# Attention plus routed feed-forward on one core: query and key stacks turned by DMA instead of by TensorE, with a fourth score bank and a new order of work

## Chip, cores and metric

One core of one Trainium2 chip. The metric is the device time of one execution in microseconds, the median of several runs. Before the change it is 717.38 us (three runs, 717.0 to 717.58).

## The reference, cut to what matters

x is 16 batches of 128 tokens with 512 numbers each; the context has 16 x 128 rows of 256.

```python
def xattn(x, ctx, pos):                      # 32 heads of 16
    q = rope(x @ Wq, pos); k, v = split(ctx @ Wkv); k = rope(k, pos)
    w = softmax(einsum('bqhd,bkhd->bhqk', q, k) / sqrt(16))
    return einsum('bhqk,bkhd->bqhd', w, v).reshape(b, n, 512) @ Wout + bout
def ffn(x):                                  # 16 experts of 352, the best 2 taken, and a shared one
    return shared(x) + sum(combine[:, e] * swiglu(x, w1[e], w3[e], w2[e]) for e in range(16))
x = x + xattn(layernorm(x), ctx, pos)
x = x + ffn(layernorm(x))
```

## The kernel before, in words

The kernel has two stages. The first handles attention, one batch of 128 tokens after the other. The second is the feed-forward part: 16 shared tiles of 128 rows, then the rows sorted by expert. The change is in the first stage, and in what the second takes over from it.

Every factor of a product in half precision is held as two f16 numbers, a high part and a low part, whose sum is the f32 value. A projection (`product`, L485) is therefore three matmuls for each 128 rows of depth. For the scores the same is done in another way. Each head has 16 numbers; `parts` holds for each head a stack of 64: for a query head high, low, high, low, for a key head high, low, low, high. The product of the two stacks over depth 64 gives all four partial products at once. The stacks lie with the tokens on the partitions and must be turned, so that the depth lies on the partitions: two heads (2 x 64) make one block of 128 x 128. There are 16 blocks for the queries and 16 for the keys of a batch.

How the stacks come about before the change, for each batch:

- `q_turn`, `q_sum` and `k_turn`, `k_sum` (VectorE, L1067 to L1091) apply the rotary embedding from the PSUM bank `p_qk` into `rot`.
- `q_high`, `k_high` (ScalarE, L793, L800) write the high part, 128x512. `q_low`, `k_low` (GpSimd, L1461 and L1466) write the low part, 128x512.
- `q_double`, `k_double` (GpSimd, L1471 and L1477) copy both parts to their second places: one instruction of 128x1024, and two of 128x512.
- `stack_transpose` (TensorE, L524), four times a batch, turns 8 blocks into the bank `p_st`. `qT_copy` twice and `kT_copy` once (ScalarE, L807, L813) and `kT_copy` once (VectorE, L1093) take them from there into `qT` and `kT`, 128x1024 each.

Then `scores` (L539) forms the scores of 8 heads at a time in two PSUM banks, `row_max` (VectorE, L1099) takes the row maxima, `negmax_transpose` (L554) turns them, `shifted_scores` (L559) forms the scores again, turned and with the maximum subtracted, `exp` (ScalarE, L820) writes the probabilities, `weigh_values` (L574) multiplies them with the values and sums them, `sums_invert` and `normalise` (VectorE, L1114, L1120) divide, and `project_out` (L601) applies Wout. The scores go through three banks: bank 0 for all even groups of heads, banks 1 and 2 by turns for the odd ones (`p_scored`, L289). So a pair of groups must wait until the pair before it has left bank 0.

The order of the work is written out by hand. Each engine has a function `step(b, on)`, and `on(d, part)` runs a part for batch b+d. `pipeline` (L297) calls it for b = 0, 1, 2, ... (from 6 on as a loop). The engines work through their lists in order and wait for each other by semaphores. Before the change TensorE is at batches b to b-4 in one step, with the scores of a batch begun at the end of step b+1 and finished in step b+2. SyncE issues the loads of the context and the stores of the normalised rows and their turned copies (`store_xn2`, `store_xn2T`).

`qT`, `kT` and `parts` exist once, so turning batch b+1 has to wait until `shifted_scores` of batch b has read the same half of `qT` and `kT`.

## Time and profile before

| | |
|---|---|
| median of three runs | 717.38 us (717.0 to 717.58) |
| the profiled execution, its own time | 722.21 us |
| its span, first to last instruction | 720.2 us |
| mean granted TensorE clock in it | 0.987 of full speed |
| attention stage, until the last output projection | about 357 us |
| feed-forward stage | about 363 us |
| PE / DVE / ACT / POOL busy, share of the span | 94% / 73% / 55% / 51% |

PE is TensorE's matmuls, PEld its weight loads, DVE VectorE, ACT ScalarE, POOL GpSimd, SP SyncE; a q behind an engine (SPq) is its queue of DMA issues. A row of a group gives the line, the engine, the operation, what is written and read, how often, the busy time and the mean of one, and then how long the engine sat idle before it and who released it. Matmuls of TensorE overlap, so the time that a block of them takes is read from the start of the block to the start of the next one, not from its duration.

### The profile page before, as it was taken

How to read it: one execution, taken by the hardware profiler on the slowest of the kernel's cores; microseconds unless marked ns; L12 is line 12 of the kernel's file. 1: busy time of each engine (PE TensorE's matmuls, PEld its weight loads, DVE VectorE, ACT ScalarE, POOL GpSimd, SP SyncE). 2: the span in 40 equal slices, each digit the busy share in tenths (PEclk: the TensorE clock that was granted, in tenths of full speed). 3: DMA queues.
4: the chain of work that ended last, by engine and by line, in shares of the span. 5: the costliest groups of instructions: out<-in, count | busy, mean ns of one | idle time of the engine just before them, and what ended most of it. 6: DMA issues, size and time to landing. Idle time of an engine off the chain costs nothing.

```text
span 720.2 us, 20582 instructions
## 1 busy us (share of the span) xinstructions
PE 675.9 (94%) x7616; PEld 435.0 (60%) x7616; DVE 522.3 (73%) x992; ACT 399.7 (55%) x668; POOL 365.9 (51%) x438
## 2 busy tenths in 40 slices
PE   3589999999999999998999999999999899999992
PEld 1356666666666666666655656666666466666661
DVE  8678888888888888876647773776767567667671
ACT  4365566666666656657531111666666456666661
POOL 4645655565556655554200001355765667777662
PEclk9999999999999999999999999999999999999997
DMA  8440111100001110100032274286587774445952
GB/s 281 174 137 1 39 39 40 39 36 17 28 30 36 36 36 29 58 29 32 32 117 88 75 278 153 74 232 165 105 261 222 207 206 86 82 85 107 263 114 32
DMA packets 37698, 73.89 MB, mean 103 GB/s; under 512 B 4048, under 2 KB 8144, under 8 KB 37648
## 3 DMA queue, kind: packets, MB, share of 16 engines
q1 hardware_dynamic: 26736, 48.81, 19.4%
q0 software_dynamic: 8752, 20.71, 15.2%
q10 hardware_dynamic: 2160, 3.69, 1.7%
q8 instruction: 33, 0.54, 0.3%
q14 instruction: 17, 0.14, 0.1%
HBM read 69.85 MB, written 22.81 MB: 129 GB/s over the span
## 4 chain that ended last, share of the span: by engine, by line
PE 83%; DMA 7%; DVE 3%; issue 3%; POOL 1%; ACT 1%; POOLq 0%; SPq 0%; DVEq 0%
PE p_sc L717 13%; PE p_qk L686 12%; PE p_st L686 11%; PE p_v L488 9%; PE p_qk L488 8%; PE p_pv L588 5%; PE p_st L536 4%; PE p_pv L591 4%; PE p_sc L568 3%; PE p_sc L551 3%; PE p_pv L598 2%; PE p_tr L680 2%; DMA stream<-x 2%; PE p_pv L704 2%; PE p_sc L571 2%
## 5 line engine op out<-in xcount | busy, mean ns | idle before, releaser
L824 ACT ACTIVATE prob<-p_sc 128x512 f32<-128x512 f32 x128 | 71.4, 601 | 53.7 <-PE p_sc L571 53.7
L1105 DVE TENSOR_REDUCE negmax<-p_sc 128x4 f16<-128x512 f32 x128 | 82.6, 684 | 6.2 <-PE p_sc L551 5.6
L946 ACT CAST hiddenT<-p_pv 128x384 f16<-128x384 f32 x54 | 25.9, 479 | 106.6 <-PE p_pv L704 104.1
L1510 POOL COPY from_at<-from_rows 128x1 uint32 (+1 forms) x40 | 33.3, 833 | 81.1 <-DVE from_rows L1351 77.8
L1530 POOL DMA_INDIRECT out<-prob,to_at x38 | 68.5, 1803 | 11.5 <-issue 10.9
L717 PE MATMUL p_sc<-used_twice,hiddenT 128*128 128x512 f16 (+1 forms) x306 | 72.9, 384 | 1.0 <-DVE hiddenT L1236 1.0
L686 PE MATMUL p_qk<-used_twice,xeT 128*128 128x352 f16 x420 | 68.4, 313 | 0.6 <-DMA xeT<-xn2T_dram 0.6
L686 PE MATMUL p_st<-used_twice,xeT 128*128 128x352 f16 x420 | 68.4, 312 | 0.0
L1232 DVE TENSOR_TENSOR hidden<-p_st,act_g 128x352 f32<-128x352 f32 x55 | 28.8, 524 | 52.9 <-PE p_st L686 32.4
L931 ACT COPY xeT<-p_tr 128x1024 f16<-128x1024 f16 x40 | 40.5, 1012 | 36.9 <-PE p_tr L680 34.3
L1249 DVE TENSOR_SCALAR prob<-p_sc,gate_at 128x512 f32<-128x512 f32 x38 | 28.6, 751 | 37.3 <-PE p_sc L717 33.8
L686 PEld LDWEIGHTS p_st<-used_twice,xeT 128*128 128x128 f16 x420 | 40.9, 98 | 21.3
L1491 POOL TENSOR_TENSOR xn_parts<-xn,xn_parts 128x512 f16<-128x512 f32 x16 | 18.5, 1158 | 69.0 <-ACT xn_parts L851 69.0
L588 PE MATMUL p_pv<-prob,used_twice_too 128*32 128x128 f32 x1024 | 52.8, 278 | 0.5 <-DVE attn L1124 0.5
L686 PEld LDWEIGHTS p_qk<-used_twice,xeT 128*128 128x128 f16 x420 | 40.8, 98 | 19.4 <-DMA xeT<-xn2T_dram 0.9
L591 PE MATMUL p_pv<-prob,sum_row 128*32 128x128 f32 x1024 | 51.7, 274 | 0.0
L488 PE MATMUL p_qk<-used_twice,xnT 128*128 128x512 f16 x192 | 49.1, 380 | 1.3 <-DVE swp L1077 1.3
L1515 POOL DMA_INDIRECT xe<-xn_dram,from_at x40 | 44.5, 1114 | 8.2 <-issue 4.2
L717 PEld LDWEIGHTS p_sc<-used_twice,hiddenT 128*128 128x128 f16 (+1 forms) x306 | 29.2, 98 | 31.4 <-issue 2.4
L488 PE MATMUL p_v<-used_twice,attnT 128*128 128x512 f16 x192 | 47.6, 380 | 0.5 <-POOL attnT L1487 0.5
L536 PE MATMUL p_st<-ident,used_twice 128*128 128x128 f16 x512 | 40.0, 222 | 7.2 <-DVE used_twice_too L1097 3.8
L1463 POOL TENSOR_TENSOR used_twice<-rot,used_twice 128x512 f16<-128x512 f32 x16 | 18.6, 1165 | 53.4 <-ACT used_twice L798 53.4
(188 smaller groups left out, 1650.6 us busy)
## 6 DMA issues: line engine op xcount, KB each, us to landing
w<-e SPq DMA_DIRECT2D x20, 1408.0 KB
w<-e SPq DMA_DIRECT2D x20, 512.0 KB
out<-stream SPq DMA_DIRECT2D x17, 256.0 KB, 2.0
xn_dram<-xn_parts SPq DMA_DIRECT2D x16, 256.0 KB, 2.0
xn2T_dram<-xn2T SPq DMA_DIRECT2D x16, 256.0 KB, 2.0
w<-e SPq DMA_DIRECT2D x20, 192.0 KB
stream<-x SPq DMA_DIRECT2D x1, 3584.0 KB, 15.7
xeT<-xn2T_dram ACTq DMA_DIRECT2D x14, 256.0 KB, 2.7
```

Of the source, the lines that this page charges most:

```text
L488: mm = pe.matmul(to, rows[:, r_part, c, :], w[:, w_part, c, :], start=(c == 0 and r_part + w_part == 0), stop=(c == last and r_part == 1))
L536: mm = pe.transpose(p_st[:, n, :], parts[:, h:h + 2, :].rearrange("p h k -> p (h k)"), ident16[:])
L588: pe.matmul(p_pv[2 * HD * n:2 * HD * (n + 1), block], vpad[:, par, head(c, n), :], prob[:, c % RING, n * P:(n + 1) * P], start=(c % 4 == 0 ...
L591: mm = pe.matmul(pv_sum[2 * HD * n:2 * HD * (n + 1), :], sum_row[:, c % 4, :], prob[:, c % RING, n * P:(n + 1) * P], start=False, stop=(c ...
L686: mm = pe.matmul(p_out, xeT[:, u, x_part, c, :], w[:, w_part, c, at:at + INNER], start=(c == 0 and x_part + w_part == 0), stop=(c == KC - ...
L717: mm = pe.matmul(p_y[u][:], hiddenT[0:k, h_part, c, :], w[0:k, w_part, c, :], start=(c == 0 and h_part + w_part == 0), stop=(c == len(ICH) ...
L824: act.activation(prob[:, c % RING, :], p_scored(c)[:], ACT.Exp, scale=SCALE).then_inc(exp_ready, 1)
L931: act.copy(xeT[:, u], p_xT).then_inc(sems.xeT_ready, 1)
L1105: dve.tensor_reduce(negmax[:, c % 2, at:at + CH], p_scored(c)[:].rearrange("p (h t) -> p h t", t=P), AX_X, ALU.max, negate=True).then_inc( ...
L1510: pool.tensor_copy(from_at[:, par, u:u + 1], from_rows[:, bass.ds(q, 1)]).then_inc(from_copied, 1)
L1515: pool.indirect_dma_start(out=xe[:, u].rearrange("p a d -> p (a d)"), out_offset=None, in_=xn2_dram, in_offset=bass.IndirectOffsetOnAxis(a ...
L1530: pool.indirect_dma_start(out=out, out_offset=bass.IndirectOffsetOnAxis(ap=to_at[:, par, u:u + 1], axis=0), in_=ye[:, par, u], in_offset=N ...
```

## The change

- The bank `p_st` goes; the scores have four banks, two for each pair of groups, by turns. The shared feed-forward part's `p_u` moves to the fourth score bank. The turned maxima go to the bank `p_tr`, which the layernorm turns of x and of xn2 use as well.
- `stack_transpose`, `qT_copy` and `kT_copy` go. SyncE issues four transposing DMAs for each batch in their place, each 128 x 1024 f16 (256 KB), straight from `parts` to `qT` or `kT`.
- `q_high`, `k_high`, `q_low`, `k_low` write each number to both of its places at once (128x1024 out of 128x512 read twice); `q_double` and `k_double` go.
- The load of x from batch 2 on, and the loads of the shared expert's weights, are issued by ScalarE.
- The steps of all engines have a new order. Scores of a batch are taken two steps behind, shifted scores and values three, the output projection four.

The core of the diff:

```diff
-        p_st32 = ps("p_st", [P, 512])
-        p_sc = [ps(f"p_sc{n}", [P, CH * P]) for n in range(3)]
+        p_sc = [ps(f"p_sc{n}", [P, CH * P]) for n in range(4)]
+        p_neg = p_xT[:, 0, 0, :]
+        p_g, p_u, p_hT = p_qk[:, 0:INNER], p_sc[3][:, 0:INNER], p_pv[:, 0:len(ICH) * P]
...
         def p_scored(c):
-            return p_sc[1 + c // 2 % 2 if c % 2 else 0]
+            return p_sc[c // 2 % 2 * 2 + c % 2]
...
+            def turn_parts(b, par, to, ready, parts_ready, at, half):
+                sp.wait_ge(parts_ready, b + 1)
+                if later(b, 1):
+                    sp.wait_ge(shifted, b * (NCH // 2) - (2 - 2 * half))
+                sp.nop().then_inc(turning, 1)
+                heads = slice(at + HALF * half, at + HALF * (half + 1))
+                sp.dma_start_transpose(to[:, 8 * half:8 * half + 8, :], parts[:, heads, :].rearrange("p h k -> p (h k)")).then_inc(ready[half], 16)
...
             def step(b, on):
-                on(4, load_ctx)
-                on(-1, store_xn2)
-                on(-1, store_xn2T)
+                on(-2, turn_k_parts, 0)
+                on(-2, turn_q_parts, 0)
+                on(-5, store_xn2)
+                on(1, load_ctx)
+                on(-2, turn_k_parts, 1)
+                on(-5, store_xn2T)
+                on(-2, turn_q_parts, 1)
...
             def scores(b, par, cc):
                 if cc % 2 == 0:
-                    pe.wait_ge(qT_ready[cc // 2], b + 1)
-                    pe.wait_ge(kT_ready[cc // 2], b + 1)
-                if cc:
-                    pe.wait_ge(max_ready, b * NCH + (2 * cc - 1))
+                    pe.wait_ge(qT_ready[cc // 2], b * 16 + 16)
+                    pe.wait_ge(kT_ready[cc // 2], b * 16 + 16)
+                if cc >= 2:
+                    pe.wait_ge(max_ready, b * NCH + (2 * cc - 2))
                 elif later(b, 1):
-                    pe.wait_ge(exp_ready, b * NCH - 1)
+                    pe.wait_ge(exp_ready, b * NCH + (2 * cc - 2))
...
             def negmax_transpose(b, par):
                 pe.wait_ge(max_ready, b * NCH + NCH)
-                pe.wait_ge(kT_ready[1], b + 1)
+                last_xn = B if isinstance(b, int) and b + 3 > B else b + 3
+                pe.wait_ge(xnT_lo, last_xn)
...
             def shifted_scores(b, par, cc):
...
-                else:
-                    pe.wait_ge(exp_ready, b * NCH + (2 * cc - 1))
+                elif cc >= 2:
+                    pe.wait_ge(exp_ready, b * NCH + (2 * cc - 2))
```

The order of TensorE after the change, one step (d is the batch b+d): project_out(-4) 0 and 1, project_k(-1) 1, negmax_transpose(-3), project_out(-4) 2, shifted_scores(-3) 0 and 1, project_out(-4) 3, weigh_values(-3) 0 and 1, shifted_scores(-3) 2 and 3, project_q(-1) 0, spread_recip(-3) 0, project_q(-1) 1, scores(-2) 0 and 1, weigh_values(-3) 2 and 3, project_q(-1) 2 and 3, xn2_transpose(-4), project_v(-1) 0, spread_recip(-3) 1, scores(-2) 2 and 3, gate_logits(-4), project_v(-1) 1, xn_transpose(0), project_k(0) 0.

VectorE: row_max(-3) 4 to 7, q_sum(-2), xnT_low(-1), neg_copy(-3), ln1_stats(0), k_turn(-1), residual(-4), ln2_stats(-4), ln1_norm(0), sums_invert(-3) 0, k_sum(-1), normalise(-3) 0, ln2_norm(-4), row_max(-2) 0 to 3, sums_invert(-3) 1, q_turn(-1), normalise(-3) 1.

ScalarE: xnT_copy(-1), q_high(-2), exp(-3) 0 to 3, summed_v_copy(-3) 0, exp(-3) 4 to 7, xn2_high(-4), summed_v_copy(-3) 1, ctx_high(0), k_high(-1), xn2T_copy(-4), attnT_high(-3), keep_logits(-4), v_copy(-1).

GpSimd: attnT_low(-4), q_low(-2), rstd1_make(0), rstd2_make(-4), xn2_low(-4), bias_add(-2), ctx_low(0), k_low(-1).

```diff
-                act.copy(parts[:, 0:HEADS, 0:HD], rot[:, 0:DIM].rearrange("p (h d) -> p h d", d=HD)).then_inc(q_hi, 1)
+                act.copy(q_part[:, :, :, 0, :], twice_each(rot[:, 0:DIM])).then_inc(q_hi, 1)
...
-                pool.tensor_tensor(parts[:, 0:HEADS, HD:2 * HD], rot[:, 0:DIM].rearrange("p (h d) -> p h d", d=HD), parts[:, 0:HEADS, 0:HD],
-                                   ALU.subtract).then_inc(q_lo, 1)
+                pool.tensor_tensor(q_part[:, :, :, 1, :], twice_each(rot[:, 0:DIM]), q_part[:, :, :, 0, :], ALU.subtract).then_inc(q_parts, 1)
```

## Rows read from the trace of the kernel before

**Rows 1.** The page, busy time of engines: us, share of the span, instructions.

```profile
PE 675.9 (94%) x7616; PEld 435.0 (60%) x7616; DVE 522.3 (73%) x992; ACT 399.7 (55%) x668; POOL 365.9 (51%) x438
```

**Rows 2.** Busy time of engines by stretches, with granted clock, DMA share, GB/s.

```profile
core 0: us, PE busy (x) PEld busy (x) DVE busy (x) ACT busy (x) POOL busy (x), PEclk, DMA share, GB/s
...
32.00:52.00 20.00, 16.75 (x227) 9.89 (x225) 15.22 (x31) 13.01 (x23) 9.05 (x8) 0.91 0.34 116
52.00:331.00 279.00, 278.67 (x4523) 184.26 (x4520) 234.83 (x477) 176.03 (x304) 162.15 (x149) 1.00 0.09 33
...
357.00:720.20 363.20, 344.75 (x2426) 218.86 (x2424) 231.05 (x399) 180.71 (x295) 171.43 (x237) 0.98 0.56 146
```

**Rows 3.** The same view for one batch of the steady stretch.

```profile
200.00:220.00 20.00, 20.00 (x326) 13.25 (x325) 17.02 (x36) 12.56 (x22) 11.75 (x12) 1.00 0.09 33
```

**Rows 4.** The timeline of TensorE: start, us, line, operation, count.

```profile
204.23 0.23 PE L568 MATMUL p_sc<-used_twice_too 64*128 64x128 f16 x2
...
204.78 0.43 PE L588 MATMUL p_pv<-prob,used_twice_too 128*32 128x128 f32 x8
...
205.79 0.62 PE L536 MATMUL p_st<-ident,used_twice 128*128 128x128 f16 x8
206.34 0.23 PE L568 MATMUL p_sc<-used_twice_too 64*128 64x128 f16 x2
...
215.55 0.40 PE L551 MATMUL p_sc<-used_twice_too 64*128 64x128 f16 x8
215.88 0.82 PE L488 MATMUL p_v<-used_twice,ctx 128*128 128x512 f16 x3
216.54 0.61 PE L598 MATMUL p_pv<-recip,spread_to 128*128 128x128 f32 x4
```

**Rows 5.** Groups by line and shape, 100 to 300 us (ten batches).

```profile
L1105 DVE TENSOR_REDUCE negmax<-p_sc 128x4 f16<-128x512 f32 x80 | 52.0, 685 | 2.8 <-PE p_sc L551 2.4
L824 ACT ACTIVATE prob<-p_sc 128x512 f32<-128x512 f32 x80 | 44.7, 600 | 35.3 <-PE p_sc L571 35.3
...
L1475 POOL TENSOR_TENSOR used_twice<-used_twice,ones 128x1024 f16<-128x1024 f16 x10 | 21.3, 2134 | 0.8
L811 ACT COPY used_twice_too<-p_st 128x1024 f16<-128x1024 f16 x20 | 20.7, 1037 | 0.0
...
L1463 POOL TENSOR_TENSOR used_twice<-rot,used_twice 128x512 f16<-128x512 f32 x10 | 11.7, 1167 | 33.5 <-ACT used_twice L798 33.5
...
L1487 POOL TENSOR_TENSOR attnT<-attn,attnT 128x512 f16<-128x512 f32 x10 | 11.6, 1156 | 5.0 <-ACT attnT L836 5.0
...
L1097 DVE COPY used_twice_too<-p_st 128x1024 f16<-128x1024 f16 x10 | 6.9, 692 | 5.1 <-PE p_st L536 4.9
...
L798 ACT CAST used_twice<-rot 128x512 f16<-128x512 f32 x10 | 6.2, 618 | 2.0 <-DVE rot L1087 2.0
```

**Rows 6.** The page, DMA queue (packets, MB, share) and issues (KB each, us to landing).

```profile
q1 hardware_dynamic: 26736, 48.81, 19.4%
...
xn2T_dram<-xn2T SPq DMA_DIRECT2D x16, 256.0 KB, 2.0
...
stream<-x SPq DMA_DIRECT2D x1, 3584.0 KB, 15.7
xeT<-xn2T_dram ACTq DMA_DIRECT2D x14, 256.0 KB, 2.7
```

**Rows 7.** The timeline of TensorE: first scores of batches 0, 1, 15; last output projection.

```profile
32.09 0.51 PE L551 MATMUL p_sc<-used_twice_too 64*128 64x128 f16 x8
...
52.07 0.40 PE L551 MATMUL p_sc<-used_twice_too 64*128 64x128 f16 x8
...
331.09 0.40 PE L551 MATMUL p_sc<-used_twice_too 64*128 64x128 f16 x8
...
354.65 2.76 PE L488 MATMUL p_v<-used_twice,attnT 128*128 128x512 f16 x12 [0.17 <-POOL attnT L1487]
```

More of the change, by code:

```diff
@@ L283, in build, with twice_each @@
         attn_rows = attn[:].rearrange("p a n -> p (a n)").rearrange("p (c t) -> p c t", t=P)
+        q_part = parts[:, 0:HEADS].rearrange("p h (t u d) -> p h t u d", t=2, u=2)
+        k_part = parts[:, HEADS:2 * HEADS]
+        k_hi_part = bass.AP(k_part.tensor, k_part.offset, [k_part.ap[0], k_part.ap[1], [3 * HD, 2], [1, HD]])
+        k_lo_part = k_part[:, :, HD:3 * HD].rearrange("p h (t d) -> p h t d", t=2)
+        def twice_each(rows):
+            return rows.rearrange("p (h o d) -> p h o d", o=1, d=HD).broadcast_to([P, HEADS, 2, HD])
         def head(c, n):
@@ L661, in step @@
-                on(-1, stack_transpose, 0)
-                on(-2, shifted_scores, 3)
-                on(-2, spread_recip, 0)
-                on(0, xn_transpose)
-                on(-1, stack_transpose, 2)
-                on(-1, scores, 0)
-                on(-2, weigh_values, 2)
-                on(-2, weigh_values, 3)
-                on(0, project_v, 0)
-                on(-1, stack_transpose, 3)
-                on(-1, scores, 1)
-                on(0, project_v, 1)
-            pipeline(step, pe, 0, B + 1, 6, (B - 6) // 2, ahead=[xn_transpose])
+                if isinstance(b, int) and b == B + 2:
+                    pe.wait_ge(turned_q, B * 3)
+                    pe.wait_ge(lo13, KC)
+                    gate(0, 0, 0, 0, "shared")
@@ L676, in rows_transpose @@
+                on(-4, xn2_transpose)
+                on(-1, project_v, 0)
+                on(-3, spread_recip, 1)
+                on(-2, scores, 2)
+                on(-2, scores, 3)
+                if isinstance(b, int) and b == B + 2:
+                    pe.wait_ge(exp_ready, B * NCH)
+                    up(0, 0, 0, 0, "shared")
+                on(-4, gate_logits)
+                on(-1, project_v, 1)
+                on(0, xn_transpose)
+                on(0, project_k, 0)
             def rows_transpose(n, u, j):
@@ L802, in k_high @@
                 if later(b, 1):
-                    act.wait_ge(stacked[1], b)
-                    act.wait_ge(stacked[3], b)
-                act.copy(parts[:, HEADS:2 * HEADS, 0:HD], rot[:, DIM:2 * DIM].rearrange("p (h d) -> p h d", d=HD)).then_inc(k_hi, 1)
-            def qT_copy(b, par, half):
-                act.wait_ge(stacked[2 * half], b + 1)
-                if later(b, 1):
-                    act.wait_ge(shifted, b * (NCH // 2) - (2 - 2 * half))
-                act.copy(qT[:, 8 * half:8 * half + 8, :], p_st[:]).then_inc(qT_ready[half], 1)
-            def kT_copy(b, par):
-                act.wait_ge(stacked[3], b + 1)
-                if later(b, 1):
-                    act.wait_ge(shifted, b * (NCH // 2))
-                act.copy(kT[:, 8:16, :], p_st[:]).then_inc(kT_ready[1], 1)
+                    act.wait_ge(kT_ready[0], b * 16)
+                    act.wait_ge(kT_ready[1], b * 16)
+                act.copy(k_hi_part, twice_each(rot[:, DIM:2 * DIM])).then_inc(k_hi, 1)
             def exp(b, par, c):
@@ L873, in split_shared2 @@
             def split_shared2():
-                for g in range(4):
-                    act.wait_ge(stacked[g], B)
+                act.wait_ge(qT_ready[0], B * 16)
                 for c, (i, k) in enumerate(ICH):
@@ L1091, in k_sum @@
                 dve.tensor_tensor(rot[:, DIM:2 * DIM], rot[:, DIM:2 * DIM], swp[:, DIM:2 * DIM], ALU.add).then_inc(k_rot, 1)
-            def kT_copy(b, par):
-                dve.wait_ge(stacked[1], b + 1)
-                if later(b, 1):
-                    dve.wait_ge(shifted, b * (NCH // 2) - 2)
-                dve.tensor_copy(kT[:, 0:8, :], p_st[:]).then_inc(kT_ready[0], 1)
             def row_max(b, par, c):
@@ L1189, in step @@
             def step(b, on):
-                on(-2, q_turn)
+                on(-3, row_max, 4)
+                on(-3, row_max, 5)
+                on(-3, row_max, 6)
+                on(-3, row_max, 7)
                 on(-2, q_sum)
+                on(-1, xnT_low)
+                on(-3, neg_copy)
+                if isinstance(b, int) and b == B + 2:
+                    split_shared13((0, 1))
                 on(0, ln1_stats)
+                on(-1, k_turn)
                 on(-4, residual)
-                on(-2, kT_copy)
                 on(-4, ln2_stats)
```

170 lines of the change are left out of this document (62 added, 108 removed).

## The prediction

> **What bounds the kernel now.** I read the page's busy shares first: TensorE is busy 94% of the span, VectorE 73% [rows 1]. A share over the whole span mixes stages, so I cut it into stretches: from 52 to 331 us TensorE is busy 278.67 of 279 us at the full clock (2.4 GHz), and the DMA engines are nearly idle, 0.09 [rows 2]. One batch there takes 20.0 us, with 17.02 us of VectorE, 12.56 of ScalarE and 11.75 of GpSimd [rows 3]. The timeline shows TensorE going from block to block without gaps [rows 4]. So the attention stage is bound by TensorE, and VectorE comes next, 3 us behind. The feed-forward stage, from 357 us on [rows 2], gets the same instructions as before (one bank has another name); I leave its 363 us alone.
>
> **What goes.** A block of eight stack turns starts at 205.79 and the next block at 206.34: 0.55 us [rows 4]. There are four a batch, 2.2 us in all. On TensorE nothing covers them: they leave the bound itself. VectorE loses one copy of 0.69 us (L1097), ScalarE three of about 1.03 (L811 and its like), GpSimd 2.13 (L1475) and two of about 1.15, as L1463 is [rows 5].
>
> **What comes on ScalarE and GpSimd.** A high part now writes 1024 numbers from 512. The nearest rows are 0.62 us for 512 (L798) and 1.04 for 1024 (L811) [rows 5]; I take the upper, so two cost 0.8 us more, and ScalarE stands at 12.6 - 3.1 + 0.8 = 10.3 us a batch. A low part on GpSimd lies between 1.17 (L1463) and 2.13 (L1475); the upper again: 11.75 - 4.4 + 1.9 = 9.2 us. Both are hidden under TensorE's 17.8 and cost nothing by themselves.
>
> **The transposing DMAs.** The trace has none, and they decide the case. Four of 256 KB a batch. Lower bound: a plain 256 KB store lands 2.0 us after issue, a load of 256 KB into SBUF 2.7, and a long load needs 15.7 us for 3584 KB, which is 1.12 us for each 256 KB that follows another [rows 6]. So two in a row land after 2.7 + 1.1 = 3.8 us. Upper bound: a turned block has rows of 128 f16, 256 bytes; one DMA has 8 blocks x 128 rows = 1024 such rows, 64 for each of 16 DMA engines. If each row costs what a packet costs in this trace on average (19.4% of 16 x 720.2 us over 26736 packets = 84 ns [rows 6]), one DMA needs 5.4 us. I take the plain transfers, because size, queue and memory are the same and only the order of the bytes differs; the upper end stays for the range.
>
> The Trainium skill, "DMA: Bandwidth & Descriptors", section "Latency and other measured facts", gives 261 GB/s as the measured effective rate of DMA transposes; by an estimate from it 256 KB take 1.0 us, and the sum would stay as it is; no row here has such a DMA. The same skill speaks against the change in "VectorE: DVE Perf Modes", section "The three transpose paths": 390 ns for a 128x128 turn on TensorE and 1309 ns by the crossbar DMA; eight turned one after the other would by that estimate take 10.5 us a DMA, and no row here shows this either.
>
> **Do they fit in the order?** I walk one step after the change; durations from rows 3 to 5, zero is the step's start. TensorE: two parts of the projection and one of k (0.66 each, 215.88 to 216.54 [rows 4]) to 2.0; turned maxima; shifted scores 0 and 1 (0.55 each, 204.23 to 204.78) end at 3.8; values 0 and 1 (1.0 each) at 6.5; shifted 2 and 3 at 7.6; scores 0 of the next batch start at 9.4. SyncE may turn k half 0 only when shifted 1 is done (`turn_parts`), about 4.0, and q half 0 when GpSimd's low part is ready: high part from 1.0 to 2.0 on ScalarE, low part to 4.2. Both must land by 9.4, so they have 5.4 us; the plain price of 3.8 fits with 1.6 to spare. The other halves start at 7.8 and are needed at 15.0, which is looser. With a fixed part of 0.9 and D for each DMA the deadline is met up to D = 2.2 us. Each us beyond that comes twice into every step.
>
> **What is queued behind these waits.** On SyncE the stores of normalised rows, the stores of their turned copies and the context load stand behind the DMA that waits for shifted scores. The context is wanted at 12.8 of the next step, and ScalarE's next copy of turned rows at about 14, while the store goes out at 9 and lands in 2.0 [rows 6]: both cost nothing while D stays small. ScalarE issues the load of x at about 9 us, before the first copy of the layernorm; half a us of issue is covered by VectorE's weight splits.
>
> **What is late next.** VectorE now holds 17.02 - 0.6 = 16.4 us in a step of 17.8. My walk gives three near misses: the maxima's turn waits for `xnT_low`, done at 1.7, with TensorE there at 2.0; the projection waits for the low part of attnT on GpSimd (1.16 us [rows 5]), which ends about 0.3 us ahead; the first values wait for exp 1 (0.60 us each, L824 [rows 5]), which ends 0.1 us late, and exp 3 0.2 us late. The fourth score bank lets scores 0 and 1 run back to back and takes nothing off TensorE's own work. For the short waits I add 0.25 us a step: 20.0 - 2.2 + 0.25 = 18.05, say 18.1 us a batch.
>
> **The sum.** The first scores of batch 0 stand at 32.09 and those of batch 15 at 331.09 [rows 7]: 15 periods of 19.93 us. 15 x (19.93 - 18.1) = 27.5 us. At the start the old order needs 20.0 us from the scores of batch 0 to those of batch 1 [rows 7]; in the new one batch 1's scores need only finished exps of batch 0, some 15 us later by the same walk (8 us to the turned maxima, 6.7 from there to scores 0), so of the 3 us I take 2 more. From the scores of batch 15 to the last projection it is 23.6 us before [rows 7]; the work behind it is the same and I change nothing. 722.2 - 29.5 = 692.7 us for the profiled execution; the median of the runs stands 4.8 us under it, so **688 us**. Own range with small errors of the waits (none, or 0.7 us a step): 681 to 696.
>
> **Rivals.**
> - **VectorE becomes the bound.** Today it stands idle 3 us a batch in short waits for TensorE (17.02 of 20.0 [rows 3]). TensorE hid them; if they all stay, a step takes 16.4 + 3.0 = 19.4 us, and the gain is 15 x 0.5 = 8 us: 709. For it: row maxima (0.685 us each, eight a batch [rows 5]) and scores wait for each other twice a step. Against: four banks uncouple the pairs. Between, 696 to 713, lies a good part of the chance.
> - **Turned scores come late: slower.** Place: TensorE's wait on `qT_ready[0]` and `kT_ready[0]` ahead of scores 0. At D = 5.4 us, q half 0 lands at 4.0 + 0.9 + 10.8 = 15.7 instead of 9.4, so TensorE stands 6.3 us in every step: 24.2 us a batch, 717 + 15 x 4.2 = 780 us. It decides against the change from 0.9 + 2D = 5.4 + 1.9, so D = 3.2 us. Pauses also cost clock: with waits of about 2 us TensorE's granted clock was 0.91 from 32 to 52 us [rows 2], that is, part of it at 1.2 GHz. The crossbar figure of the Trainium skill's VectorE page would belong here, beyond 780.
> - **It does not do what it says:** the DMA writes turned numbers one by one, 131072 of two bytes. Even at a tenth of a packet's 84 ns that is 69 us a DMA on 16 engines, over 1000 us in all. For it speaks no row; the plain store of 256 KB in 2.0 us speaks against any such pace.
>
> **Chances.** A measurement of this kernel can tell about 0.2% (1.4 us) from no change. Forecast 0.50 (681 to 696), VectorE or an unforeseen wait 0.25 (696 to 716), break-even between the sides 0.04, late turns 0.19, not as it says 0.02. So faster 0.75, same 0.04, slower 0.21. The range reaches from 680 to 712: it holds the forecast and nearly all of the second case, and what it leaves out is mostly the slower side, 2 in 10.
>
> **What would show it.** Right: blocks of L536 gone, TensorE above 97% in the steady stretch, the period between first scores about 18.1 us, ScalarE near 10 and GpSimd near 9 us in it, transposing DMAs landing in 2 to 4 us, DMA share about 0.25 (four times 256 KB beside today's 640 KB at 0.09). Wrong in the first way: TensorE idle ahead of L551 scores or the turned maxima, released by VectorE's maxima, VectorE above 90%. Wrong in the second way: idle ahead of scores released by a DMA into `qT` or `kT`, the landing times above 3.2 us, a granted clock below 1.0 in the steady stretch, and SyncE's stores late. A feed-forward stage that changes by more than 2 us would make the argument incomplete.

## The result, and the profile after

After the change the median is 691.06 us (four runs, 689.33 to 692.89) against 717.48 for the kernel before on the same chip: ratio 0.9614, 95% interval 0.9575 to 0.9653, 26 us faster. Timed once more beside the kernel before it gave 0.9667 (0.9629 to 0.9704). Forecast were 688 us and a range of 680 to 712. The profiled execution took 689.33 us, span 687.5 us, granted clock 0.984. The medians below are of all executions of a kernel; the ratios are estimated from the fast ones alone, which leaves out one execution each of e2_q_twice, e5_small_turns and e8_old_order_ctx, and they differ from the plain quotients of the medians by up to 0.4%.

The page, busy time of the engines, answers to [rows 1]:

```profile
PE 635.5 (92%) x7104; PEld 406.6 (59%) x7104; DVE 503.2 (73%) x976; ACT 368.9 (54%) x620; POOL 332.9 (48%) x390
```

TensorE has 512 matmuls fewer (16 batches x 32 turns) and 40 us less busy time. Its share fell, although it still is the bound; the shares say little here. Busy time by stretches, as in [rows 2], and one batch, as in [rows 3]:

```profile
core 0: us, PE busy (x) PEld busy (x) DVE busy (x) ACT busy (x) POOL busy (x), PEclk, DMA share, GB/s
...
32.00:52.00 20.00, 13.36 (x200) 9.13 (x201) 15.39 (x30) 11.28 (x19) 6.03 (x4) 0.83 0.29 52
52.00:300.00 248.00, 242.42 (x4098) 158.73 (x4094) 215.27 (x463) 149.63 (x262) 132.42 (x107) 1.00 0.49 104
...
325.00:690.00 365.00, 344.28 (x2414) 218.56 (x2412) 231.01 (x399) 180.62 (x294) 172.38 (x237) 0.98 0.55 146
```

```profile
204.11:221.72 17.61, 17.55 (x295) 11.46 (x293) 15.72 (x34) 11.15 (x20) 9.78 (x8) 1.00 0.43 97
```

A batch takes 17.6 us where it took 20.0. VectorE fills 89% of it and still doesn't hold TensorE up. In the fill, 32 to 52 us, TensorE does less than before (13.36 us against 16.75). The feed-forward stage is as it was.

The timeline of TensorE, first scores of batches 0, 1 and 15 and the last output projection, as in [rows 7]:

```profile
30.86 0.62 PE L552 MATMUL p_sc<-used_twice_too 64*128 64x128 f16 x16 [0.38 <-DMA used_twice_too<-used_twice]
...
51.22 0.62 PE L552 MATMUL p_sc<-used_twice_too 64*128 64x128 f16 x16
...
298.37 0.88 PE L552 MATMUL p_sc<-used_twice_too 64*128 64x128 f16 x16
...
322.63 2.76 PE L504 MATMUL p_v<-used_twice,attnT 128*128 128x512 f16 x12 [0.33 <-POOL attnT L1450]
```

This gives the balance of the two spans (720.2 - 687.5 = 32.7 us). The first scores stand 1.2 us earlier. The 15 periods to the scores of batch 15 went from 19.93 to (298.37 - 30.86) / 15 = 17.83 us: 31.5. From there to the last projection it is 24.3 us against 23.6: -0.7. Behind it lie 364.9 against 365.5: +0.7. So the whole gain is the shorter period. (The two profiled executions lie 6.3 us further apart than the two medians, so 32.7 us is more than the 26 of the medians, and no trace tells in which stage the difference lies.) But the first of these periods, batch 0 to 1, is 20.4 us long; in the steady part ten of them (105.13 to 282.33) take 17.72 each.

Inside a step, the timeline of TensorE from 204 us, as in [rows 4] (start, us, line, operation, count):

```profile
204.91 0.23 PE L573 MATMUL p_sc<-used_twice_too 64*128 64x128 f16 x2
...
205.91 0.82 PE L504 MATMUL p_v<-used_twice,attnT 128*128 128x512 f16 x3
...
211.80 0.62 PE L552 MATMUL p_sc<-used_twice_too 64*128 64x128 f16 x16
212.35 0.43 PE L593 MATMUL p_pv<-prob,used_twice_too 128*32 128x128 f32 x8
```

Two groups of scores, 16 matmuls, now run in one block of 0.55 us. Before, each group of 8 took 0.33, as from 215.55 to 215.88 in [rows 4], so two took 0.66. Two groups of shifted scores take 1.00 us (204.91 to 205.91), before twice 0.55. With two pairs of each in a batch that is 2 x 0.11 + 2 x 0.10 = 0.4 us a batch. It stands in no term of my sum. Why a joined block is shorter, no run shows.

And the new instruction, the transposing DMA (duration on SP's queue in ns min/median/max, first and last start), with the time from issue to landing:

```profile
L425 SPq DMA_TRANSPOSE used_twice_too<-used_twice x64: 1231/1259/2214, 21.9 to 299.2; - x64
...
DMA to landing us min/median/max: 3.0/3.2/5.6
```

It holds SP's queue for 1.26 us and lands after 3.2. The first two of the step above, and a plain store for comparison, in the timeline of SP's queue:

```profile
206.09 2.62 SPq L425 DMA_TRANSPOSE used_twice_too<-used_twice  x2
209.19 0.34 SPq L405 DMA_DIRECT2D xn_dram<-xn_parts  x1
```

The second of the two, the query's half 0, is issued at about 207.4, lands by the median at about 210.6, and the scores start at 211.80. That is a slack of 1.2 us.

### The profile page after: what moved, and what is told of

Same layout as the page of the kernel before. It is cut to its first block, busy times and chain, and to the rows that moved or that the text cites. A ratio compares the mean times of both kernels' runs of the same rounds, so it can differ in the third digit from the quotient of the medians.

```text
span 687.5 us, 19434 instructions
## 1 busy us (share of the span) xinstructions
PE 635.5 (92%) x7104; PEld 406.6 (59%) x7104; DVE 503.2 (73%) x976; ACT 368.9 (54%) x620; POOL 332.9 (48%) x390
## 2 busy tenths in 40 slices
DMA packets 105279, 90.63 MB, mean 132 GB/s; under 512 B 71632, under 2 KB 75728, under 8 KB 105232
## 4 chain that ended last, share of the span: by engine, by line
PE 79%; DMA 5%; DVE 5%; issue 4%; POOL 2%; ACT 2%; SPq 2%; POOLq 0%; ACTq 0%; DVEq 0%
PE p_sc L724 14%; PE p_qk L693 13%; PE p_sc L693 12%; PE p_qk L504 8%; PE p_v L504 8%; PE p_pv L593 4%; PE p_pv L596 3%; DMA used_twice_too<-used_twice 3%; PE p_tr L687 2%; PE p_pv L711 2%; PE p_sc L552 2%; PE p_pv L603 2%; PE p_sc L573 2%; PE p_sc L576 1%; SPq L425 1%
## 5 line engine op out<-in xcount | busy, mean ns | idle before, releaser
L1085 DVE TENSOR_REDUCE negmax<-p_sc 128x4 f16<-128x512 f32 x128 | 79.4, 684 | 6.0 <-PE p_sc L552 4.6
L811 ACT ACTIVATE prob<-p_sc 128x512 f32<-128x512 f32 x128 | 66.1, 602 | 20.2 <-PE p_sc L576 19.9
L693 PE MATMUL p_sc<-used_twice,xeT 128*128 128x352 f16 x420 | 68.4, 312 | 0.0
L1211 DVE TENSOR_TENSOR hidden<-p_sc,act_g 128x352 f32<-128x352 f32 x55 | 28.8, 524 | 52.5 <-PE p_sc L693 32.0
L504 PE MATMUL p_qk<-used_twice,xnT 128*128 128x512 f16 x192 | 52.1, 399 | 6.4 <-DVE swp L1063 6.4
L1442 POOL TENSOR_TENSOR used_twice<-rot,used_twice 128x1024 f16<-128x1024 f32 x16 | 34.2, 2136 | 43.6 <-ACT used_twice L798 43.6
L693 PEld LDWEIGHTS p_sc<-used_twice,xeT 128*128 128x128 f16 x420 | 41.0, 98 | 21.4
L693 PEld LDWEIGHTS p_qk<-used_twice,xeT 128*128 128x128 f16 x420 | 40.8, 98 | 19.4 <-DMA xeT<-xn2T_dram 0.7
L724 PE MATMUL p_sc<-used_twice_too,hiddenT 128*128 128x512 f16 (+1 forms) x180 | 43.3, 386 | 0.0
```

Source lines behind the costliest of these rows:

```text
L504: mm = pe.matmul(to, rows[:, r_part, c, :], w[:, w_part, c, :], start=(c == 0 and r_part + w_part == 0), stop=(c == last and r_part == 1))
L693: mm = pe.matmul(p_out, xeT[:, u, x_part, c, :], w[:, w_part, c, at:at + INNER], start=(c == 0 and x_part + w_part == 0), stop=(c == KC - ...
L724: mm = pe.matmul(p_y[u][:], hiddenT[0:k, h_part, c, :], w[0:k, w_part, c, :], start=(c == 0 and h_part + w_part == 0), stop=(c == len(ICH) ...
L811: act.activation(prob[:, c % RING, :], p_scored(c)[:], ACT.Exp, scale=SCALE).then_inc(exp_ready, 1)
L1085: dve.tensor_reduce(negmax[:, c % 2, at:at + CH], p_scored(c)[:].rearrange("p (h t) -> p h t", t=P), AX_X, ALU.max, negate=True).then_inc( ...
L1442: pool.tensor_tensor(q_part[:, :, :, 1, :], twice_each(rot[:, 0:DIM]), q_part[:, :, :, 0, :], ALU.subtract).then_inc(q_parts, 1)
```

## The experiments

Two measures for all of them: the ratio to the kernel before, timed beside it on the same chip, with its interval, and the period, taken as the distance from the first to the last turning of the maxima (`negmax_transpose`) over 15. By that measure the kernel before has (339.2 - 38.7) / 15 = 20.03 us and the change 17.65. A period is that of the one profiled execution, which can lie several us from the median: that of the kernel before lies 4.7 us above it, those of e2, e5, e4, e8 and e9 8, 12, 7, 7 and 4 us above theirs. A few us over 15 batches are some tenths of a us of period.

| run | what it is | median us | ratio to before | period us |
|---|---|---|---|---|
| change | first timing | 691.06 | 0.9614 (0.9575 to 0.9653) | 17.65 |
| e0_change | the change, timed once more | 692.96 | 0.9667 (0.9629 to 0.9704) | 17.61 |
| e1_turns_back | change, TensorE's 32 turns back in | 713.6 | 0.9891 (0.9822 to 0.996) | 19.08 |
| e2_q_twice | change, one DMA repeated | 746.66 | 1.0365 (1.03 to 1.0431) | 21.39 |
| e3_three_banks | e6 with three banks | 735.91 | 1.0294 (1.0263 to 1.0324) | 20.91 |
| e4_dma_only | old order, three banks, doubling, DMA turns | 725.29 | 1.0072 (1.0034 to 1.0109) | 20.20 |
| e5_small_turns | change, each DMA in two halves | 738.3 | 1.0264 (1.0213 to 1.0315) | 21.15 |
| e6_wo_later | change, one weight split a step later | 688.98 | 0.9582 (0.9539 to 0.9625) | 17.81 |
| e6b_wo_later | the same again, beside e0 | 689.26 | 0.961 (0.9576 to 0.9645) | 17.79 |
| e7_double_kept | change, doubling kept | 703.76 | 0.9812 (0.9779 to 0.9845) | 18.43 |
| e8_old_order_ctx | e4, context loaded earlier | 713.36 | 0.9959 (0.9929 to 0.9989) | 19.51 |
| e9_old_order_once | e8, both places written at once | 703.66 | 0.9794 (0.9754 to 0.9834) | 18.63 |
| e10_wo_early_act | e6, ScalarE's half of the split earlier | 689.76 | 0.959 (0.9542 to 0.9639) | 17.83 |

**e1_turns_back: what are the turns worth?** Four blocks of eight turns of the identity, whose results nobody reads, are put back on TensorE.

```diff
+            def idle_turns(bank):
+                for n in range(8):
+                    pe.transpose(bank[:].bitcast(F16)[:, n * P:(n + 1) * P], ident16[:], ident16[:])
...
+                if c == 0:
+                    idle_turns(p_qk)
```

> The changed kernel with 32 turns of 128x128 a batch put back on TensorE (of the identity, into p_qk and p_v ahead of four projections, results overwritten). Theory A (the gain is the turns' own time on TensorE, the engine that bounds): a batch takes 17.7 + 2.2 = 19.9 us and the time goes to 720 to 724 us, that is, the whole gain or a little more is gone. Rival B (the gain comes from the new order and the fourth bank; the turns fit beside VectorE's work): at most 700 us.

It came out between the two: 713.6 us. The period is 1.43 us longer than the change's. A block of eight, read in the timeline of TensorE of this run:

```profile
208.30 0.62 PE L510 MATMUL p_qk<-ident 128*128 128x128 f16 x8
208.76 0.81 PE L504 MATMUL p_qk<-used_twice,xnT 128*128 128x512 f16 x3
```

That is 0.46 us, so four of them are 1.8 us of TensorE's time, of which 1.4 are seen. The turns carry most of the gain, but not all of it: with as many turns as before the kernel is still 1.1% faster (20.03 to 19.08 us). This rest is not of the new order and the fourth bank alone, for here ScalarE and VectorE still have no copies out of `p_st` to do, and GpSimd no doubling.

**e3_three_banks: is the fourth bank needed?** The version of e6 (below), with the old assignment of banks and its waits.

```diff
-            return p_sc[c // 2 % 2 * 2 + c % 2]
+            return p_sc[1 + c // 2 % 2 if c % 2 else 0]
...
-                if cc >= 2:
-                    pe.wait_ge(max_ready, b * NCH + (2 * cc - 2))
-                elif later(b, 1):
-                    pe.wait_ge(exp_ready, b * NCH + (2 * cc - 2))
+                if cc:
+                    pe.wait_ge(max_ready, b * NCH + (2 * cc - 1))
+                if cc < 2 and later(b, 1):
+                    pe.wait_ge(exp_ready, b * NCH - 1 + cc)
...
-                elif cc >= 2:
-                    pe.wait_ge(exp_ready, b * NCH + (2 * cc - 2))
+                else:
+                    pe.wait_ge(exp_ready, b * NCH + (2 * cc - 1))
```

> The kernel of the run before this one (split one step later) with three score banks in place of four: scores 1 must wait for the maxima of scores 0, shifted scores 1 and 3 for an exp each. Theory A (the fourth bank is what lets the new order put pairs of scores together): TensorE waits about 1 us behind scores 0, 1 us behind shifted 0 and as much in the other pairs, 3 to 4 us a batch, 735 to 750 us. Rival B (the bank only saves the switch between blocks, 0.1 us each): 690 to 697 us.

735.91 us, as theory A had it. What TensorE waits for between 100 and 280 us (us in total, times, longest):

```profile
PE p_sc L552 <- DVE negmax L1085: 14.3, 17, 1.1
PE p_sc L573 <- ACT prob L811: 13.1, 17, 1.1
```

The pairs stand back to back in the new order. With bank 0 shared by all even groups the second group of a pair waits for the maxima, or for the exp, of the first: 27.4 us in 180, some 3 us a batch. So the bank has no gain of its own that could be added up; it is what makes the new order possible.

**e4_dma_only, e8_old_order_ctx, e9_old_order_once: the DMA turns without the new order.** First only the turning is left to the DMAs, in the kernel before.

```diff
-                on(4, load_ctx)
-                on(-1, store_xn2)
-                on(-1, store_xn2T)
+                on(-4, store_xn2)
+                on(1, load_ctx)
+                on(-4, store_xn2T)
+                on(-1, turn_parts, kT, kT_ready, HEADS, 0)
+                on(-1, turn_parts, qT, qT_ready, 0, 0)
+                on(-1, turn_parts, kT, kT_ready, HEADS, 1)
+                on(-1, turn_parts, qT, qT_ready, 0, 1)
```

> The kernel before, with its own order, three score banks and the doubling on GpSimd kept; only the stack turns and their copies are replaced by the four transposing DMAs a batch (and the loads of x and the shared weights are issued as in the change). Theory A (the gain is the removed TensorE work, whatever the order): 17.9 to 18.3 us a batch, 685 to 697 us. Rival B (the old order and its three banks cannot use the freed time): 19.3 us or more a batch, 707 us or more.

Slower than before, 725.29 us, though TensorE has 2.2 us less to do in each batch. Both numbers are in the range of rival B, but its cause, the order and its three banks, is not what this trace shows (e8 and e9 test it). Waits from 100 to 280 us:

```profile
PE p_sc L541 <- DMA used_twice_too<-used_twice: 7.9, 8, 1.5
ACT ctx L830 <- DMA ctx_sb<-ctxT: 6.1, 9, 0.8
...
PE p_v L493 <- ACT used_twice_too L776: 4.3, 9, 0.7
```

The second row is a fault of my edit: the context load comes late, ScalarE waits for it, and the copy of the values, for which TensorE waits in the third row, comes behind. What holds the load up in SP's queue are not the transposing DMAs, as I had taken it, but the store of the normalised rows ahead of it, which waits for GpSimd. The timeline of SP's queue, first of e4, then of e8:

```profile
193.52 7.95 SPq L420 DMA_TRANSPOSE used_twice_too<-used_twice  x4
205.68 0.34 SPq L397 DMA_DIRECT2D xn_dram<-xn_parts  x1
206.31 0.41 SPq L409 DMA_DIRECT2D ctx_sb<-ctxT  x1
```

```profile
204.73 7.41 SPq L420 DMA_TRANSPOSE used_twice_too<-used_twice  x4
212.47 0.41 SPq L409 DMA_DIRECT2D ctx_sb<-ctxT  x1
216.26 0.35 SPq L397 DMA_DIRECT2D xn_dram<-xn_parts  x1
```

In e4 the last transposing DMA has left the queue at 201.5 us and the load goes out at 206.31, right behind the store. e8 issues that load a batch earlier, still behind the transposing DMAs but ahead of the store.

```diff
-                on(1, load_ctx)
...
+                on(2, load_ctx)
...
+            load_ctx(2, 0)
```

> The kernel before in its own order with its three banks and its doubling, only the turning left to the DMAs, as in the run of that name; here the context of the next batch is also loaded a step earlier, because in that run ScalarE waited 0.7 us a batch for this load, which stood behind the transposing DMAs in SP's queue. Theory A, the place of the load was what made that run no faster: 712 us or less, a period of 19.0 us or less. Theory B, the chain query parts, doubling, transposing DMA, scores is what binds in the old order, and the load was hidden or nearly so: 718 to 725 us, TensorE still waits for the transposing DMA in front of the scores, some 0.8 us a batch.

713.36 us: the late load was 1.1% of the time. The time is nearer to theory A (712 or less), the period of 19.51 us is not (19.0 or less), and the wait that theory B names is there, so both were in part right. The wait of the scores stays, at the same size:

```profile
PE p_sc L542 <- DMA used_twice_too<-used_twice: 9.9, 9, 1.4
```

One step of e8, GpSimd, then TensorE (its SP queue stands above, the four issues from 204.73 us):

```profile
204.54 1.17 POOL L1431 TENSOR_TENSOR used_twice<-rot,used_twice 128x512 f16<-128x512 f32 x1 [3.13 <-ACT used_twice L784]
205.79 2.14 POOL L1443 TENSOR_TENSOR used_twice<-used_twice,ones 128x1024 f16<-128x1024 f16 x1
...
211.30 0.40 PE L542 MATMUL p_sc<-used_twice_too 64*128 64x128 f16 x8 [0.79 <-DMA used_twice_too<-used_twice]
```

The low part of the query ends at 205.7, the doubling at 207.9, the transposing DMA issued then lands by the median 3.2 us later, at 211.1, and 0.2 us after that the scores start. e9 removes the doubling: both places are written at once, as in the change.

```diff
-                pool.tensor_tensor(parts[:, 0:HEADS, HD:2 * HD], rot[:, 0:DIM].rearrange("p (h d) -> p h d", d=HD), parts[:, 0:HEADS, 0:HD],
-                                   ALU.subtract).then_inc(q_lo, 1)
+                pool.tensor_tensor(q_part[:, :, :, 1, :], twice_each(rot[:, 0:DIM]), q_part[:, :, :, 0, :], ALU.subtract).then_inc(q_parts, 1)
...
-                on(-2, q_double)
```

> The run just named (old order, three banks, DMA turns, early context load) with both places of the parts written at once by ScalarE and GpSimd, so that no doubling stands between the query's low part and its turning. Theory A, that chain binds: it is 1.2 us a batch shorter, the wait in front of the scores goes, and the time is 705 to 715 us. Theory B, the old order binds by itself (three banks, the scores right behind the projections they depend on): the same as the run just named within 3 us.

703.66 us: theory A, a little below its range. From 100 to 280 us no scores wait for a DMA any more; the nearest are short waits of the shifted scores for an exp (1.8 us in all, 4 times). Somewhat over half of the gain of the change (2.1% of 3.3 to 3.9%) is therefore to be had in the old order with three banks: DMA turns and writing at once are worth 20.03 - 18.63 = 1.40 us a batch. From e9 to the change only the order of work and the bank differ: 18.63 - 17.65 = 0.98 us. That e1 leaves 0.95 looks like a second measure of the same, but it is of other parts, as said above, and the executions of e9 alone reach from 698.66 to 707.52 us, which would be 0.6 us a batch if it all lay in the attention stage. The two numbers agree closer than they can be known.

**e7_double_kept: writing at once, in the new order.**

```diff
+                on(-2, q_low)
+                on(-2, q_double)
...
+                on(-1, k_low)
+                on(-1, k_double)
```

> The changed kernel with the high and low parts written once and doubled on GpSimd as before (its busy time a batch 9.8 + 2.3 us, its chain from the sum to the finished parts 1.2 us longer for queries and 1.2 us longer for keys, behind which the low part of attnT stands). Theory A (writing both places at once is needed to land the turns in time: the cover was 1.2 us, and attnT's low part had 0.3 us): 0.7 to 1.5 us more a batch, 701 to 714 us. Rival B (GpSimd has 7 us to spare, so the doubling is hidden): under 694 us.

703.76 us, theory A in size. What TensorE waits for, 100 to 280 us:

```profile
PE p_v L504 <- POOL attnT L1466: 6.1, 9, 0.8
PE p_pv L593 <- ACT prob L811: 1.4, 5, 0.4
```

The wait is not where e9 has its gain. Here it is the output projection that waits, for the low part of attnT, which GpSimd reaches late behind the doubling. The same doubling hurts the query's turning in the old order and the output projection in the new one.

**e2_q_twice and e5_small_turns: how much slack have the transposing DMAs?** In e2 the first query half is turned twice, the second time after the first has landed.

```diff
+                if at == 0 and half == 0:
+                    sp.dma_start_transpose(to[:, 8 * half:8 * half + 8, :], parts[:, heads, :].rearrange("p h k -> p (h k)")).then_inc(turned_once, 16)
+                    sp.wait_ge(turned_once, b * 16 + 16)
```

> The changed kernel, but SyncE turns query half 0 twice, the second time after the first has landed. In the changed kernel that half lands about 1.2 us before TensorE starts scores 0, and a turning DMA lands 3.2 us after its issue. Theory A (scores 0 wait on that DMA once the slack is used): scores 0 come about 2 us late in every step, 19.8 us a batch, 715 to 725 us. Rival B (DMA turns have ample cover, as the walk with 1.6 us to spare and looser later halves suggests): under 695 us.

746.66 us, worse than both expectations. Yet the delay was as expected. Two issues of the query's half 0, in the timeline of SP's queue, and the scores that wait for the second:

```profile
205.52 1.26 SPq L426 DMA_TRANSPOSE used_twice_too<-used_twice  x1
208.66 1.23 SPq L429 DMA_TRANSPOSE used_twice_too<-used_twice  x1
...
211.85 0.62 PE L556 MATMUL p_sc<-used_twice_too 64*128 64x128 f16 x16 [1.89 <-DMA used_twice_too<-used_twice]
```

The two issues stand 3.1 us apart; less the slack of 1.2 that is a wait of 1.9 us. From 100 to 280 us such waits stand ahead of the scores of every batch, 20.5 us in 9 waits, seven of them between 1.8 and 2.1 us and two longer. What I had left out is the clock. Two batches that follow each other, from scores to scores, in the columns of the stretches above (the granted clock is the third number from the end):

```profile
192.27:211.85 19.58, 17.63 (x294) 11.41 (x295) 15.81 (x34) 10.83 (x19) 9.91 (x9) 1.00 0.45 101
211.85:233.02 21.17, 19.15 (x293) 12.91 (x294) 15.75 (x34) 10.82 (x19) 9.73 (x9) 0.92 0.42 93
```

At the full clock a batch takes 19.6 us, which is 17.7 and the wait of 1.9, near the 19.8 expected. In the other the granted clock is 0.92, a part of it ran at 1.2 GHz, and the same work takes 1.6 us more. Why the clock falls behind every other of these waits, though all are of nearly the same length, no run shows. This profiled execution was the slowest of its four (754.33 us, granted clock 0.945), but the other three had 0.951 to 0.958 too, against 0.976 to 0.984 in those of the change.

In e5 each DMA is cut in two of four blocks, with the same bytes.

```diff
+                for n in range(2):
+                    heads = slice(at + HALF * half + 8 * n, at + HALF * half + 8 * n + 8)
+                    sp.dma_start_transpose(to[:, 8 * half + 4 * n:8 * half + 4 * n + 4, :], parts[:, heads, :].rearrange("p h k -> p (h k)")).then_inc(ready[half], 16)
```

> The changed kernel with each transposing DMA cut in two of four blocks (8 a batch instead of 4, the same bytes and the same blocks). Theory A, the 1.25 us of the SP queue are paid by the block (0.16 us each): an issue of a half takes about 0.63 us, the last key and query rows land when they did, and the time stays at 691 us within 2 us. Theory B, they are paid by the DMA: an issue still takes about 1.25 us, the SP queue holds eight of them, 10 us a batch, the last query half is issued 2.5 us later than in the changed kernel, whose slack there was 1.2 us, so 1.3 us a batch or more: 710 us or above.

738.3 us, theory B. The DMA's own row, and the time from issue to landing:

```profile
L427 SPq DMA_TRANSPOSE used_twice_too<-used_twice x128: 1188/1253/2247, 22.2 to 355.8; - x128
...
DMA to landing us min/median/max: 2.4/2.5/5.1
```

Half the bytes take the same 1.25 us of the queue and land 0.7 us sooner. Eight issues are 10 us of SP's queue in a batch. And the wait comes twice, ahead of both pairs of scores, 25.5 us in 180, with about 0.7 us ahead of the one pair and 2 us ahead of the other:

```profile
PE p_sc L554 <- DMA used_twice_too<-used_twice: 25.5, 17, 3.1
```

**e6_wo_later and e10_wo_early_act: the fill.** In the profile of the change the longest idle time of TensorE between the first and the second scores ends at 42.55 us; the timeline of all engines:

```profile
35.52 2.18 ACT L850 ACTIVATE used_twice<-w 128x512 f16<-128x512 f32 x4
36.17 2.50 DVE L1046 SCALAR_TENSOR_TENSOR used_twice<-w,used_twice 128x512 f16<-128x512 f32 x4 [1.13 <-ACT used_twice L850]
...
38.72 2.48 DVE L1085 TENSOR_REDUCE negmax<-p_sc 128x4 f16<-128x512 f32 x4
41.11 0.69 DVE L1073 TENSOR_TENSOR rot<-rot,swp 128x512 f32<-128x512 f32 x1
41.71 0.69 DVE L1041 TENSOR_TENSOR xnT<-p_tr,xnT 128x512 f16<-128x512 f32 x1
...
42.55 0.27 PE L562 MATMUL p_tr<-ident,negmax 128*128 128x128 f16 x1 [5.83 <-DVE xnT L1041]
```

VectorE splits the output weights (2.5 us, and 1.1 us of waiting for ScalarE) ahead of the maxima. TensorE's granted clock was 0.55 in the 5.5 us behind this pause, so most of them ran at 1.2 GHz:

```profile
42.50:48.00 5.50, 4.72 (x93) 4.32 (x97) 3.86 (x9) 3.73 (x6) 3.89 (x3) 0.55 0.32 64
```

e6 puts that split one step later.

```diff
+                if isinstance(b, int) and b == 3:
+                    weights_low(wo16, wo_in, KC, KCC + KC)
...
-                if isinstance(b, int) and b == 2:
-                    weights_low(wo16, wo_in, KC, KCC + KC)
```

> The changed kernel with the split of the output weights on VectorE moved from the end of step 2 to step 3, where the residual of a later batch would stand. Theory A (in the filling of the pipeline TensorE waits 5.8 us for VectorE, of which the split is 3.5 us): first maxima turned about 3.5 us earlier, 686 to 689 us. Rival B (the fill is bound by something else, the loads or the chain of the first two batches): no change within 1 us.

> The changed kernel itself once more, on the same chip as the next three, as their measure. Both theories: ratio to the kernel before 0.957 to 0.965, about 18 us a batch early on and 17.7 later.

> The output weights' split moved one step later on VectorE, beside the changed kernel on one chip. In the first run the first maxima came 2.2 us earlier, but from the fourth batch on the profile stood level with the changed kernel's, because the DMA turns of the early batches were late. Theory A (the fill gain lasts): 1.5 to 3 us below the changed kernel. Rival B (the early steps wait for the DMA turns anyway, so the gain is taken back): within 1 us of it.

The first maxima are turned at 40.3 us instead of 42.5, and in the second pair (e6b beside e0) at 41.9 instead of 45.1; theory A of e6 had said 3.5 us. The last are turned at 307.4 and 308.8, where the change has 307.2 and 309.3: what the fill gains is mostly lost again on the way. The medians are 0.3% and 0.5% below those of the change, with intervals that overlap. The 3.7 us between the medians of e6b and e0 are more than theory A's 1.5 to 3, and the profiles show 0.5 of them at the last maxima. The change itself came out at 0.9667, just above the 0.957 to 0.965 expected of it.

e10 also moves ScalarE's half of the split to where ScalarE stood idle (25.8 to 33.2 us).

> The changed kernel with VectorE's half of the output weights' split one step later, as in the run of that name, and ScalarE's half of it moved ahead of the key parts of batch 1, where ScalarE stood idle from 25.8 to 33.2 us. Theory A, the fill (the stretch from the first to the second scores) is bounded by ScalarE's split, which holds back the copy of batch 2's normalised rows until 40.5 us: the first maxima are turned 1.5 to 2 us earlier than in that run (near 40 instead of 41.9 us), and all later ones too: 687 us against 689. Theory B, another thing bounds the fill (the key projection, or the landing of the first transposing DMAs): within 0.5 us of that run.

By the time it is theory B, 689.76 us against 689.26 of e6b, though the first maxima are turned at 41.0, 0.9 us ahead of e6b. The copy of the turned rows by ScalarE comes 2 us sooner (38.50 instead of 40.48), but VectorE's `xnT_low` now stands behind row maxima and the query's rotary sum, and VectorE is busy without a pause from 35.89 us, where it had waited 0.6 us for a projection. e6, e6b and e10 lie at 0.958 to 0.961, the two timings of the change at 0.961 and 0.967. A gain of a few us from the later split is likely; no interval separates it.

## Why the prediction was right, and where it was not

The mechanism held: turns leave TensorE, which is the bound, and the DMAs land in time. The median came 3 us above the forecast, in the range. That it came so near is in part luck: against the sum, the 14 later periods were 6.3 us shorter, the first one 4.3 us longer, and the step from one execution to the median was off by 6.5 us. The smaller rest is in the edges (first scores 1.2 us earlier, the end of the stage 0.7 us later, the feed-forward stage 0.7 us shorter).

- **The period, 18.1 forecast, 17.72 measured.** The term "takes nothing off TensorE's own work", said of the fourth bank, failed: back to back, the pairs save 0.4 us a batch, which the timeline shows. 20.0 - 2.2 - 0.4 is 17.4; the 0.3 that are left are about the short waits, for which I had 0.25. TensorE's idle time fits: it was busy 242.42 of 248 us, 0.4 us idle a batch, where before it was 278.67 of 279. e1 puts the turns at 1.4 us in the new order, less than the 2.2 of my first step: those blocks are shorter (0.46 us each), and 0.4 of their 1.8 us do not show in the period.
- **The fill, 16.1 us forecast from the first scores of batch 0 to those of batch 1, 20.4 measured.** (The sum had 18.1, less 2.) The step "batch 1's scores need only finished exps of batch 0, some 15 us later" was a walk of the steady order. In the fill VectorE and ScalarE also split the output weights, and TensorE stood 5.83 us in one piece; ScalarE had stood 6.41 us before that, until 32.33 us, for a transposing DMA. The granted clock from 32 to 52 us was 0.83 instead of 0.91, so more of it ran at 1.2 GHz. I had looked at the work of a step and not at what is only done once, inside it.
- **From one execution to the median.** I took 4.8 us off because the profiled execution of before stood that far above its median. That of after is the fastest of its four, 1.7 us under its median. The forecast for the profiled execution was 692.7 and it took 689.3; the forecast for the median was 688.0 and it is 691.1. The offset belongs to one execution and cannot be carried over.
- **The price of a transposing DMA** lay near the lower bound. My reason, the same size, queue and memory, is not shown by that: the plain store goes to DRAM and this DMA stays in SBUF, and it holds the queue longer (1.26 us against 0.34) and lands later (3.2 against 2.0) than that store. Two in a row land (207.4 + 3.2) - 206.1 = 4.5 us after the first issue; the plain price said 3.8, the upper bound 11.7. Of the 1.6 us of slack 1.2 were there. In "VectorE: DVE Perf Modes", section "The three transpose paths", the Trainium skill has 1309 ns for a 128x128 turn by the crossbar DMA; the trace does not agree if that is taken block after block, for eight land 3.2 us after issue; a DMA of one block was not run.
- **A late turn.** "Each us beyond that comes twice into every step" holds where both halves are late (e5, 17 waits in 180 us), not where one is (e2, 9 waits). The walk named the right place, and the price of a late landing was real: 1.9 us of lateness cost 1.9 us of period where the clock stayed full, and 3.5 where it fell to 0.92 (e2). The margin of 1.2 us is thin. That pauses also cost clock stood in the prediction, without a price.
- **VectorE as the bound** (the first rival) did not come: 15.7 of 17.6 us busy, and its short waits shrank with the period. It had been put at 19.4 us a step. VectorE also had less to do than the 16.4 us of the forecast, and not by the copy alone. In the kernel before, every second scaling of normalised rows (`xn`) ran beside a doubling of GpSimd and took twice as long. The timelines of VectorE and GpSimd before, then of VectorE after:

```profile
211.70 0.54 DVE L1026 TENSOR_SCALAR xn<-stream,mv,rstd 128x512 f32 x1
220.90 1.09 DVE L1026 TENSOR_SCALAR xn<-stream,mv,rstd 128x512 f32 x1
...
220.56 1.15 POOL L1483 TENSOR_TENSOR used_twice<-used_twice,ones 128x512 f16<-128x512 f16 x1
...
211.60 0.54 DVE L1012 TENSOR_SCALAR xn<-stream,mv,rstd 128x512 f32 x1
```

  From 100 to 300 us all ten that overlap L1483 took 1.08 or 1.09 us and all ten others 0.54; in the change all take 0.54 to 0.55, also in e7, where the doubling is kept but falls elsewhere. That is half a us of VectorE a batch, which no term of mine had.
- **Near misses.** Of the three that the walk gave, the low part of attnT binds as soon as GpSimd has more work (e7); exp 1 and 3 cost 1.4 us in 180 (`p_pv` after `prob`), the turned maxima nothing in the steady part.
- **Smaller sizes.** ScalarE 11.15 us a batch for 10.3, GpSimd 9.78 for 9.2, DMA share 0.49 for 0.25. The last was estimated by bytes. The DMA's packets are small: (105279 - 37698) / 64 = 1056 for each DMA, about the 1024 rows of 256 bytes that I had counted.
- **The feed-forward stage** stayed within 0.6 us.

What no run settles: how the 0.98 us of new order and bank divide into joined pairs (0.4 by the timeline) and better overlap.

## What to carry to other kernels

Moving work off the bound engine pays only if what takes its place is ready when it is asked for: the same DMA turns were 0.7% slower, 0.4% faster and 2.1% faster in the old order, by where a load stood in a queue and by a doubling on another engine. So measure a change of several parts both ways, each part alone and each part left out; here the fourth bank, which my sum gave nothing, is worth 3 us a batch in the new order. And walk the fill with its one-time work, not with the steady step. A pause of the bound engine costs more than its length where its clock falls (e2): 1.9 us of waiting and, in every other batch of its steady part, 1.6 us more for the same work.

## What the hardware showed that I had not expected

- A transposing DMA holds the issuing queue for 1.25 us, with 8 blocks of 128x128 as with 4 (e5), against 0.34 for a plain store of 256 KB. From issue to landing it is 3.2 us for 256 KB and 2.5 for 128 KB.
- It keeps the DMA engines busy beyond its bytes, but less than its packets would in the mean. The page's queues with packets, MB and share of 16 engines' span:

```profile
q1 hardware_dynamic: 91600, 59.76, 33.4%
...
q10 hardware_dynamic: 4880, 9.52, 4.1%
```

  Before, these two had 19.4% [rows 6] and 1.7%. That is 37.5% of 16 x 687.5 us against 21.1% of 16 x 720.2 us, 1694 us more for 64 DMAs: 26.5 us of DMA engine for each, 1.7 us on each of the 16, and 25 ns for each packet, where the mean packet of before took 84. This takes the other transfers as unchanged.

- TensorE's busy share does not tell the period. From 100 to 200 us e9 and the change are busy alike, but one gets through 7% more matmuls of the same kinds (its period is 5% shorter; some records can be missing):

```profile
100.00:200.00 100.00, 98.66 (x1579) 60.64 (x1581) 85.80 (x188) 57.72 (x104) 49.30 (x42) 1.00 0.44 90
```

```profile
100.00:200.00 100.00, 98.42 (x1689) 65.18 (x1688) 88.61 (x192) 61.12 (x108) 54.54 (x46) 1.00 0.49 103
```

The first row is of e9, the second of the change. The ends of matmuls are modelled in the records, so short waits and switches between blocks can hide in them; the distance between two starts of the same instruction is what to read.
